# Four-layer attention and feed-forward kernel: the first feed-forward layer is computed in pieces inside the attention steps, through the two PSUM banks that the small products share

## The chip, the cores and the metric

The kernel runs on one core of a Trainium2 chip. The metric is the device time of one execution in microseconds (us). A core has a matrix engine (TensorE, PE in the profile, with its weight loads as PEld), VectorE (DVE), ScalarE (ACT), GpSimd (POOL) and SyncE (SP, which here issues all transfers). Each engine takes its own instructions strictly in order and waits on semaphores for the others. Matrix products land in PSUM, eight banks of 128 x 512 floats, and DVE or ACT take them out from there.

## The reference, cut to what matters

The input x has 4 batches of 512 tokens of 128 channels. Every layer adds an attention and then a feed-forward network to x, each on the layer norm of x:

```
x = x + attention0(norm(x))   # 16 heads of 8, keys: 154 of the context and 64 learned ones
x = x + ffn0(norm(x))
x = x + attention1(norm(x))   # keys and queries RMS-normalised, 154 keys
x = x + ffn1(norm(x))         # 4 experts of 512, gated
x = x + attention2(norm(x));  x = x + ffn2(norm(x))
x = x + attention3(norm(x));  x = x + ffn3(norm(x))

def ffn0(x):                  # per batch; m1, m2: outer products of 16 tokens' rows
    h = gelu(x @ (W1 + scale * m1(x)).T + b1)     # 128 -> 512
    return h @ (W2 + scale * m2(x)).T + b2        # 512 -> 128
```

The weights of ffn0 differ from batch to batch, because m1 and m2 are made of 16 token rows of the normalised x of that batch. What one batch does never depends on another batch.

## The kernel before

The work is a list of 32 items, layer by layer and batch by batch: four attention items A of layer 0, four of ffn0 (kind F0), four A of layer 1, four F1, four A of layer 2, four F2, A3, F3. In this text A0 to A3 are the attention items of layer 0, A4 to A7 those of layer 1, A8 to A11 those of layer 2, and F0_0 to F0_3 are the four batches of ffn0.

An item has slots (steps). An attention item has N = 28 slots in layer 0 and N = 20 in the layers 1 and 2, and four more in which its last products drain. In slot n `attention_step` has PE compute one block of transposed scores into bank 0 or 1 (L819), ACT takes its exp into a ring of eight (`exps`, L1534), and from slot 5 on PE runs, every fourth slot each, four products of the probabilities with the values into bank 6 (L830) and four for the denominators into bank 7 (L838). Scores of slot n wait for the exp of slot n-2, which read the same bank. At the end DVE takes a reciprocal and multiplies (`attention_end`), and the output product and its addition to x are the piece "finish", in slot 6 of the next item.

What else an item needs is done in pieces within the slots of the items ahead of it. `plan(i)` writes them down: `put(n, name, ...)` hangs a piece on slot n of item i, and every engine walks through the slots in order and, in a slot, first does the item's own step and then the slot's pieces in the order of the put calls. The pieces of this text: "ln" and "norm" (layer norm: statistics on DVE, the rest on POOL), "xt" (four PE transposes into bank 4, copied out by ACT, L698, L1445), "q", "q1" to "q4", "qsplit", "qlow" (query projection and its preparation; "q1" and "q3" on POOL, "q2" and "q4" on DVE), "kproj", "k1", "k2", "k3", "ksplit", "klow" (the same for the keys; "k2" on DVE, "k1", "k3", "klow" on POOL, "ksplit" on ACT), "kt" (transposes of the keys into the banks 4 and 5), "kb" (four ACT copies out of both banks, one per head of a group, L1426), "qxt" (four groups g of query transposes into bank 2 + g%2, each copied out by ACT, L720, L1473), "max" (32 score products m into bank 2 + m%2, each reduced by DVE, L736, L1118), "mt" (the transposed maxima), "v" (values, part 0 in bank 4 and part 1 in bank 5, masked out of PSUM by DVE). For each bank the builder keeps in `taken` which signal frees it. PE waits for that signal before the bank's next product, and all that stands behind it in PE's queue waits too.

```
            for h in range(HL):
                put(h, "kb", a1, h)
            for g in range(G):
                put(1 + g, "qxt", a1, g)
            for m in range(N_MAX):
                put(5 + m * (N - 4) // N_MAX, "max", a1, m)
```

An F0 item has 4 slots and 4 for the drain. "rows": SP copies the 16 rows of xn into `EV`/`OD` with four DMAs (`lora_dma`) and POOL spreads them (`lora_rows`). "late": PE makes m1 and m2 by two products into bank 5 (`lora`, L768), DVE adds each to the weights (L1192, L1194), ACT and DVE split the first into two parts of fp32r. Then `up` (three products per tile of 128 hidden channels, L874 to L876, into the banks 0 and 2), gelu on ACT (L1551), and `down` (16 products of 128 columns, L893, bank 6 or 7), which DVE adds to x (L1293). While the F0 items run, no attention item does: in their slots lie the preparation of A4 and A5 and all 32 "max" of A4.

Of the kernel before, what the change touches and what calls it, by code (L numbers as in the profile page):

```python
# [116 lines left out]

def plan(i):

# [9 lines left out]
    a = layer * B + b  # L129
    nxt = i + 1  # L130
    if i + 2 < len(ITEMS) and ITEMS[i + 2][0] == "A" and ITEMS[i + 2][2] == 0:
        put(0, "bv", ITEMS[i + 2][1])
    if i + 2 < len(ITEMS):
        for t in range(T):
            put(0 if kind in ("F0", "A3", "F3") else t, "ln", i + 2, t)
        put(0 if kind in ("F0", "A3", "F3") else 3, "norm", i + 2)
    if kind == "A":
        if is_attn(nxt):
            a1 = a + 1
            if b == 0:  # L140
                put(0, "kt", a1)
            for h in range(HL):
                put(h, "kb", a1, h)
            for g in range(G):
                put(1 + g, "qxt", a1, g)
            for m in range(N_MAX):
                put(5 + m * (N - 4) // N_MAX, "max", a1, m)
            put(6 + (N_MAX - MT_LAST) * (N - 4) // N_MAX, "mt", a1, 0)
            put(N + 1, "mt", a1, 1)
            put(N, "v", a1, 0)  # L150
            put(N + 1, "v", a1, 1)
        if is_attn(i + 2):
            put(N + 3, "kt", a + 2)
        if is_ffn(nxt):
            put(2, "xt", nxt)
            put(3, "after_xt", nxt)
            for n in range(3):
                put(5 + n, "late", nxt, n)
        if is_attn(i - 1):
            put(6, "finish", i - 1)  # L160
        if is_attn(i + 2):
            put(7, "xt", i + 2)
            put(9, "q", a + 2)
            for n, name in ((9, "q1"), (11, "q2"), (12, "q3"), (16, "q4"), (17, "qsplit"), (18, "qlow")):
                put(n, name, a + 2)
        if a + 2 < 12:
            put(10, "kproj", a + 2)
            for n, name in ((10, "k1"), (12, "k2"), (13, "k3"), (N - 2, "ksplit"), (N - 1, "klow")):
                put(n, name, a + 2)
        if i + 2 < len(ITEMS) and ITEMS[i + 2][0] == "F0":  # L170
            put(10, "rows", i + 2)
        if layer > 0:
            n_w = len(weight_chunks(layer))
            for c in range(b * n_w // B, (b + 1) * n_w // B):
                put(4 + 3 * (c - b * n_w // B), "w", layer, c)
    elif kind in ("F0", "F1", "F2"):
        short = kind == "F0"
        if is_attn(i - 1):
            put(2, "finish", i - 1)
# [22 lines left out]
        if is_attn(i + 2):  # L202
            a2 = ITEMS[i + 2][1] * B + ITEMS[i + 2][2]
            at = (3, 3, 3, 4, 4, 5, 6, 7) if short else (5, 6, 6, 7, 7, 8, 8, 9)
            for n, name in zip(at, ("xt", "q", "q1", "q2", "q3", "q4", "qsplit", "qlow")):
                put(n, name, i + 2 if name == "xt" else a2)
        if i + 2 < len(ITEMS) and ITEMS[i + 2][0] == "F0":
            put(N, "rows", i + 2)
# [1676 lines left out]
```

## Time and profile before

| | us |
|---|---|
| median of three runs (lowest, highest) | 1090.92 (1089.46, 1092.05) |
| the profiled execution, whole | 1092.3 |
| its span, first to last instruction | 1090.4 |
| PE busy in the span | 962.9 |
| DVE / ACT / POOL busy | 572.2 / 432.6 / 270.5 |
| first scores of A1 to first scores of A6 | 293.4 |

The profile is one execution seen instruction by instruction. A timeline row gives the start, the duration, the engine, the source line, what is written and read, how many instructions of one kind are merged, and, in brackets, how long the engine sat idle before and who released it. The duration of matrix products overlaps with that of the next ones, so what one costs is read from the distance of the starts. PEclk is the clock that TensorE was granted, 1.00 being 2.4 GHz; it has two levels, and a mean between 0.5 and 1.0 says what part of a stretch lay at the lower one, 1.2 GHz.

### The profile page before, as it was taken

What the parts mean: (1) busy time and instruction counts of PE and PEld (TensorE: products, weight loads), DVE (VectorE), ACT (ScalarE), POOL (GpSimd) and SP (SyncE); (2) the same over time, 40 slices, a digit from 0 to 9 for tenths busy, and PEclk for the clock granted to TensorE, in tenths of its full rate; (3) what the DMA queues carried; (4) which work ended last, traced back from release to release, by engine and by line L of the source; (5) the groups of instructions that cost most, each with busy time, mean ns of one, the idle gap of its engine ahead of it and who ended that gap; (6) DMA issues with size and microseconds to landing.
All of it is one profiled execution on the core that took longest, in us unless ns stands there. A gap on an engine that the chain in (4) does not pass through costs nothing. (4 is left out here: it accounts for less than half of the span.)

```text
span 1090.4 us, 15279 instructions
## 1 busy us (share of the span) xinstructions
PE 962.9 (88%) x5522; PEld 659.4 (60%) x5522; DVE 572.2 (52%) x1371; ACT 432.6 (40%) x777; POOL 270.5 (25%) x394
## 2 busy tenths in 40 slices
PE   2788989988689888899998889898899999999885
PEld 2544454335554443478887655444488888878783
DVE  3645555433355656455454636757453645444468
ACT  1355554442326554433333244654522423222340
POOL 7311212334425451311021023521200101010044
PEclk9989999787769999999999989989999999999997
DMA  5000000000010111000000020110000000000001
GB/s 142 4 2 13 1 15 2 13 8 10 1 63 8 33 33 32 1 22 1 1 1 1 1 73 21 39 40 15 19 1 1 1 1 1 1 1 1 1 1 39
DMA packets 27572, 18.09 MB, mean 17 GB/s; under 512 B 6221, under 2 KB 25770, under 8 KB 27370
## 3 DMA queue, kind: packets, MB, share of 16 engines
q1 hardware_dynamic: 27498, 17.12, 5.6%
q8 instruction: 45, 0.74, 0.3%
q14 instruction: 29, 0.24, 0.1%
HBM read 15.63 MB, written 1.05 MB: 15 GB/s over the span
## 5 line engine op out<-in xcount | busy, mean ns | idle before, releaser
L1118 DVE TENSOR_REDUCE mneg<-PS 128x2 f32<-128x308 f32 (+1 forms) x384 | 184.0, 517 | 161.6 <-PE PS L736 155.6
L1534 ACT ACTIVATE work<-PS 124x512 f32<-124x512 f32 (+1 forms) x272 | 160.4, 605 | 135.2 <-PE PS L819 134.4
L1266 DVE TENSOR_TENSOR work<-PS,work 128x512 f32<-128x512 f32 (+2 forms) x168 | 114.8, 685 | 175.5 <-PE PS L876 129.8
L1559 ACT ACTIVATE work<-PS 128x512 f32<-128x512 f32 (+2 forms) x168 | 100.1, 597 | 253.3 <-PE PS L876 240.9
L893 PEld LDWEIGHTS PS<-down_w,work 128*128 128x128 f32 (+2 forms) x1472 | 174.6, 193 | 6.2 <-DVE work L1266 1.3
L893 PE MATMUL PS<-down_w,work 128*128 128x128 f32 (+2 forms) x1472 | 174.8, 276 | 1.0 <-DVE work L1266 1.0
L874 PE MATMUL PS<-xh_sb,arena 128*128 128x512 f32 (+2 forms) x352 | 148.7, 422 | 10.4 <-DVE work L1266 9.6
L1629 POOL TENSOR_SCALAR rstd<-bn_mv 128x4 f32<-128x4 f32 x32 | 8.7, 271 | 537.7 <-DVE bn_mv L1038 537.6
L876 PE MATMUL PS<-xh_sb,arena 128*128 128x512 f32 (+2 forms) x352 | 141.7, 403 | 0.0
L875 PE MATMUL PS<-xl_sb,arena 128*128 128x512 f32 (+2 forms) x352 | 141.0, 400 | 0.0
L736 PE MATMUL PS<-kb_sb,qxt_sb 97*128 97x308 f32 x256 | 88.6, 394 | 19.6 <-DVE mneg L1118 14.9
L736 PEld LDWEIGHTS PS<-kb_sb,qxt_sb 97*128 97x128 f32 x256 | 47.1, 198 | 95.2 <-DVE mneg L1118 52.0
L874 PEld LDWEIGHTS PS<-xh_sb,arena 128*128 128x128 f32 (+2 forms) x352 | 65.6, 186 | 35.5 <-DVE work L1266 14.1
L830 PE MATMUL PS<-work,vb_sb 124*32 124x512 f32 (+1 forms) x544 | 76.7, 637 | 2.9 <-DVE work L1241 1.8
L819 PE MATMUL PS<-qxt_sb,kb_sb 101*124 101x512 f32 x160 | 72.4, 469 | 5.7 <-ACT work L1534 5.6
L876 PEld LDWEIGHTS PS<-xh_sb,arena 128*128 128x128 f32 (+2 forms) x352 | 65.5, 186 | 18.3
L838 PE MATMUL PS<-work,mv_sb 124*32 124x512 f32 (+1 forms) x544 | 74.6, 621 | 0.0
L875 PEld LDWEIGHTS PS<-xl_sb,arena 128*128 128x128 f32 (+2 forms) x352 | 65.9, 187 | 12.8
L1239 DVE RECIPROCAL work<-PS 128x512 f32<-128x512 f32 x12 | 40.3, 3357 | 41.0 <-PE PS L838 41.0
L1297 DVE SCALAR_TENSOR_TENSOR x_res<-PS,gates_sb,x_res 128x128 f32<-128x128 f32 x192 | 53.5, 339 | 5.9 <-PE PS L893 5.9
L736 PE MATMUL PS<-arena,qxt_sb 97*128 97x436 f32 x128 | 48.8, 423 | 7.2 <-DVE mneg L1118 6.1
L736 PEld LDWEIGHTS PS<-arena,qxt_sb 97*128 97x128 f32 x128 | 22.9, 189 | 51.1 <-DVE mneg L1118 33.7
(169 smaller groups left out, 1209.7 us busy)
## 6 DMA issues: line engine op xcount, KB each, us to landing
ctx_rep<-in_ctxT SPq DMA_DIRECT2D x12, 308.0 KB, 3.2
stage<-in_w SPq DMA_DIRECT2D x8, 256.0 KB, 3.6
stage<-in_wg SPq DMA_DIRECT2D x8, 176.0 KB, 2.4
stage<-in_wu SPq DMA_DIRECT2D x8, 176.0 KB, 2.9
x_res<-in_x SPq DMA_DIRECT2D x4, 256.0 KB, 4.0
down_w<-in_w SPq DMA_DIRECT2D x1, 1024.0 KB
down_w<-in_wd SPq DMA_DIRECT2D x8, 128.0 KB
out<-x_res SPq DMA_DIRECT2D x4, 256.0 KB, 2.3
```

The costliest lines, as they stand in the source:

```text
L736: pe.matmul(PS[:, bank, 0:w], QXT[0:KX_ROWS, a % 2, g, t * 128:(t + 1) * 128], KB(layer)[0:KX_ROWS, a % 2, g, f * w:(f + 1) * w], start=Tr ...
L819: pe.matmul(PS[0:rows, n % 2, :], KB(layer)[0:K_ALL, a % 2, g, c * rows:(c + 1) * rows], QXT[0:K_ALL, a % 2, g, :], start=True, stop=True) ...
L830: pe.matmul(PS[32 * g:32 * g + 32, 6, :], VB[0:rows, a % 2, c, g * 32:(g + 1) * 32], P[0:rows, (4 * c + g) % P_RING, :], start=(c == 0), s ...
L838: pe.matmul(PS[32 * g:32 * g + 32, 7, :], mask[0:rows, c, :], P[0:rows, (4 * c + g) % P_RING, :], start=(c == 0), stop=(c == chunks - 1)). ...
L874: pe.matmul(o, w[0], xH[:, i % 2, :], start=True, stop=False)
L875: pe.matmul(o, w[0], xL[:, i % 2, :], start=False, stop=False)
L876: pe.matmul(o, w[1], xH[:, i % 2, :], start=False, stop=True).then_inc(*sig["up"].mark((i, kt, m)))
L893: mm = pe.matmul(PS[:, bank, t * 128:(t + 1) * 128], HH[0:rows, bank - 6, j, t * 128:(t + 1) * 128], rhs, start=(j == 0), stop=(j == len(t ...
L1118: dve.tensor_reduce(mneg[:, a % 2, t, h0:h0 + 2], PS[:, mx_bank(i_main, m), 0:2 * (KT0 if layer == 0 else KC)].rearrange("p (h n) -> p h n ...
L1266: dve.tensor_tensor(HH[0:rows, e % 2, j, :], PS[0:rows, 2 * (n % 2) + 1, :], SS[0:rows, n % 2, :], ALU.mult).then_inc(*sig["h"].mark((i, n)))
L1534: act.activation(P[0:rows, n % P_RING, :], PS[0:rows, n % 2, :], ACT.Exp, scale=SCALE).then_inc(*sig["p"].mark((i, n)))
L1559: act.activation(SS[0:rows, n % 2, :], PS[0:rows, bank, :], ACT.Silu).then_inc(*sig["act"].mark((i, n)))
```

## The change

The F0 items vanish from the walk (`MAIN` is the list of items without them) and their work becomes pieces of attention slots. For the batch b: "ln" and "norm" in the slots 9 and 10, "rows" in 13, "xt" in 16, "late" in 20 of the item A(b+1); "up0" (one tile each, into bank 4 or 5) in its slots N and N+1, one later for b = 3; "down0" (one quarter each, into bank 5) in the slots 1 to 4 and "acc0" in slot 4 of A(b+2). The layer norm of A(4+b) follows in the slots 4 and 5 of A(b+2), its "xt" in 9, "q" and "q1" in 11, "q2", "q3" in 16, "q4" in 20. In the items A2 to A5 the key pieces "k2" and "k3" go from 12 and 13 to 15 and 16, "ksplit" and "klow" from N-2 and N-1 to N and N+1. A3 now prepares A4 as every attention item prepares the next.

In all attention items that are followed by another, of every layer, "kb" goes from the slots 0 to 3 to the slots 0, 0, 1, 1, and "qxt" from the slots 1 to 4 to 2, 3, 5, 6. "max" stays from slot 5 on.

Buffers are made apart so that both can run: hidden layer `HH0`, `LW` for m1's sum, `EO` and `EBD` for the rows; `W1E` moves within the arena; the two buffers of the layer norm are dealt by the new order (`ring`) rather than by the item number's parity. The loads of later weights are issued at other items, and DMA scratch is set to 1024.

```diff
+    if is_attn(nxt):
+        a1 = a + 1
+        if a in (0, 2 * B):
+            put(0, "kt", a1)
+        for h in range(HL):
+            put(h // 2, "kb", a1, h)
+        for g in range(G):
+            put((2, 3, 5, 6)[g], "qxt", a1, g)
+        first = 5
+        for m in range(N_MAX):
+            put(first + m * (N + 1 - first) // N_MAX, "max", a1, m)
...
+        put(N + 1, "mt", a1, 1)
+        put(N, "v", a1, 0)
+        put(N + 1, "v", a1, 1)
+    if is_attn(nxt2):
+        put(N + 3, "kt", a + 2)
...
+    if is_attn(after(i, -1)):
+        put(6, "finish", after(i, -1))
+    for b0 in range(B):
+
+        j = B + b0
+        for t in range(T):
+            put_later(b0 + 1, 9, "ln", j, t)
+        put_later(b0 + 1, 10, "norm", j)
+        put_later(b0 + 1, 13, "rows", j)
+        put_later(b0 + 1, 16, "xt", j)
+        put_later(b0 + 1, 17, "after_xt", j)
+        put_later(b0 + 1, 20, "late", j, 0)
+        for n in range(4):
+            put_later(b0 + 1, n_slots(item_of(b0 + 1)) + (b0 == 3) + n // 2, "up0", j, n)
+        for t in range(T):
+            put_later(b0 + 2, 1 + t, "down0", j, t)
+        put_later(b0 + 2, 4, "acc0", j)
+        n = B + b0
+        for t in range(T):
+            put_later(b0 + 2, 4, "ln", item_of(n), t)
+        put_later(b0 + 2, 5, "norm", item_of(n))
+        for x, name in ((9, "xt"), (11, "q"), (11, "q1"), (16, "q2"), (16, "q3"), (20, "q4"), (21, "qsplit"), (22, "qlow")):
+            put_later(b0 + 2, x, name, item_of(n) if name == "xt" else n)
...
+        put(10, "kproj", a + 2)
+        for n, name in ((10, "k1"), (15 if shared else 12, "k2"), (16 if shared else 13, "k3"), (N if shared else N - 2, "ksplit"), (N + 1 if shared else N - 1, "klow")):
+            put(n, name, a + 2)
...
+            def up0(i, n):
+
+                b, bank = ITEMS[i][2], 4 + n % 2
+                if n == 0:
+                    pe.wait_ge(*sig["xl"].at(i))
+                    pe.wait_ge(*sig["lora_l"].at(i))
+                pe.wait_ge(*taken[bank])
+                cols = slice(n * 128, (n + 1) * 128)
+                pe.matmul(PS[:, bank, :], W1E[:, b % 2, 0, cols], xH[:, i % 2, :], start=True, stop=False)
+                pe.matmul(PS[:, bank, :], W1E[:, b % 2, 0, cols], xL[:, i % 2, :], start=False, stop=False)
+                pe.matmul(PS[:, bank, :], W1E[:, b % 2, 1, cols], xH[:, i % 2, :], start=False, stop=True).then_inc(*sig["up"].mark((i, n, 0)))
+                taken[bank] = sig["h_gelu"].at((i, n))
+
+            def down0(i, t):
+
+                b = ITEMS[i][2]
+                if t == 0:
+                    pe.wait_ge(*sig["h_gelu"].at((i, 3)))
+                    pe.wait_ge(*sig["lora_w"].at((i, 1)))
+                    pe.wait_ge(*taken[5])
+                for j in range(4):
+                    mm = pe.matmul(PS[:, 5, t * 128:(t + 1) * 128], HH0[:, j, t * 128:(t + 1) * 128], W2E[:, b % 2, j * 128:(j + 1) * 128],
+                                   start=(j == 0), stop=(j == 3))
+                if t == T - 1:
+                    mm.then_inc(*sig["y"].mark((i, 0)))
+                    taken[5] = sig["resid"].at(i)
...
+            def accumulate0(i):
+
+                b = ITEMS[i][2]
+                dve.wait_ge(*sig["y"].at((i, 0)))
+                dve.wait_ge(*sig["bias_in_x"].at(i))
+                xb = x[:, b * T:(b + 1) * T, :]
+                dve.tensor_tensor(xb, PS[:, 5, :].rearrange("p (t n) -> p t n", t=T), xb, ALU.add).then_inc(*sig["resid"].mark(i))
...
+            def gelu(i, n):
+
+                act.wait_ge(*sig["up"].at((i, n, 0)))
+                if n == 0:
+                    act.wait_ge(*sig["w_ffn0_in"].at(0))
+                    if ITEMS[i][2] > 0:
+                        act.wait_ge(*sig["y"].at((i - 1, 0)))
+                act.activation(HH0[:, n, :], PS[:, 4 + n % 2, :], ACT.Gelu, bias=b1T[:, n:n + 1]).then_inc(*sig["h_gelu"].mark((i, n)))
```

## Rows read from the trace of the kernel before

**Rows 1.** The page: busy time of the matrix engine, its share and instructions.

```profile
PE 962.9 (88%) x5522; PEld 659.4 (60%) x5522; DVE 572.2 (52%) x1371; ACT 432.6 (40%) x777; POOL 270.5 (25%) x394
```

**Rows 2.** Windows: A1, A2, A3, F0 with A4's preparation, A4, A5.

```profile
core 0: us, PE busy (x) PEld busy (x) DVE busy (x) ACT busy (x) POOL busy (x), PEclk, DMA share, GB/s
...
102.58:148.93 46.35, 42.69 (x258) 21.32 (x256) 26.92 (x48) 23.61 (x43) 7.39 (x9) 0.96 0.03 8
148.93:192.18 43.25, 39.35 (x237) 18.77 (x236) 26.41 (x49) 22.19 (x40) 12.56 (x24) 1.00 0.03 7
192.18:228.70 36.52, 33.30 (x164) 10.74 (x160) 11.47 (x19) 17.54 (x33) 12.89 (x24) 0.81 0.03 10
228.70:322.73 94.03, 71.79 (x313) 51.17 (x309) 41.29 (x95) 27.45 (x43) 35.24 (x52) 0.74 0.03 7
322.73:359.68 36.95, 34.71 (x200) 19.01 (x200) 20.71 (x54) 20.25 (x37) 19.15 (x38) 0.91 0.14 50
359.68:395.95 36.27, 32.49 (x202) 16.89 (x200) 24.14 (x55) 20.14 (x37) 19.10 (x38) 1.00 0.08 25
```

**Rows 3.** Timeline of PE in the F0 stage: down, up, the two `lora` products.

```profile
244.54 3.73 PE L893 MATMUL PS<-down_w,work 128*128 128x128 f32 x32
248.03 0.48 PE L874 MATMUL PS<-xh_sb,arena 128*128 128x512 f32 x1
...
248.90 1.12 PE L768 MATMUL PS<-stage,qb_sb 4*128 4x512 f32 x2
251.25 1.12 PE L768 MATMUL PS<-stage,qb_sb 4*128 4x512 f32 x2 [1.24 <-DVE qa_sb L1192]
252.31 0.50 PE L874 MATMUL PS<-xh_sb,arena 128*128 128x512 f32 x1
```

**Rows 4.** Timeline of PE at the head of A5: slots 0, 5, 7.

```profile
359.68 0.71 PE L819 MATMUL PS<-qxt_sb,kb_sb 101*124 101x512 f32 x2
...
365.70 1.06 PE L830 MATMUL PS<-work,vb_sb 124*32 124x512 f32 x8
366.70 0.41 PE L736 MATMUL PS<-kb_sb,qxt_sb 97*128 97x308 f32 x1
...
369.44 0.48 PE L819 MATMUL PS<-qxt_sb,kb_sb 101*124 101x512 f32 x1
```

**Rows 5.** Timeline of PE: transposes, and the product that needs ACT's copy of them.

```profile
293.97 0.63 PE L698 MATMUL PS<-ident_sb,xn_sb 128*128 128x128 f32 x4 [0.24 <-DVE mneg L1118]
295.38 2.05 PE L708 MATMUL PS<-w_attn,xt_sb 128*128 128x128 f32 x8 [0.78 <-ACT xt_sb L1445]
```

**Rows 6.** Timeline of ACT at the head of A5.

```profile
360.69 0.77 ACT L1426 ACTIVATE kb_sb<-PS,maskk_sb 97x616 fp32r<-97x616 f32 x1
...
361.82 0.79 ACT L1426 ACTIVATE kb_sb<-PS,maskk_sb 97x616 fp32r<-97x616 f32 x1
```

**Rows 7.** Timeline of DVE: last seed of "q2" in A4; first "max" in A5.

```profile
343.23 0.19 DVE L428 TENSOR_SCALAR q_rr_sb<-q_ms_sb 128x64 int32<-128x64 int32 x1
...
367.15 0.48 DVE L1118 TENSOR_REDUCE mneg<-PS 128x2 f32<-128x308 f32 x1 [2.28 <-PE PS L736]
```

**Rows 8.** Timeline of POOL: `lora_rows` in F0; end of "k3" in A4; norm in A5.

```profile
256.09 1.03 POOL L1735 TENSOR_TENSOR stage<-qb_sb,eye_sb 4x512 f32<-4x512 f32 x1 [5.02 <-DMA qb_sb<-xn_sb]
...
353.73 0.20 POOL L1686 COPY kx_sb<-kbias 77x8 f32<-77x8 f32 x1
...
364.96 0.23 POOL L1629 TENSOR_SCALAR rstd<-bn_mv 128x4 f32<-128x4 f32 x1 [9.11 <-DVE bn_mv L1038]
...
367.51 1.04 POOL L1636 TENSOR_TENSOR xn_sb<-xn_sb,rstd 128x512 f32<-128x512 f32 x1
```

**Rows 9.** Timeline of ACT: the switch from exp to gelu.

```profile
228.98 1.28 ACT L1551 ACT_TABLE_LOAD   x1 [2.19 <-PE PS L838]
230.28 0.69 ACT L1551 ACTIVATE work<-PS,b1t 128x512 f32<-128x512 f32 x1
```

**Rows 10.** Timeline of PE at the head of A6, which starts at 395.95.

```profile
404.51 0.55 PE L736 MATMUL PS<-kb_sb,qxt_sb 97*128 97x308 f32 x2
```

More of the change, by code:

```diff
@@ L65, with after, norm_order, ring @@
 ITEMS = [(kind, n // 2, b) for n, kind in enumerate(KINDS) for b in range(B)]
+MAIN = [i for i, item in enumerate(ITEMS) if item[0] != "F0"]
+def after(i, n):
+    p = MAIN.index(i) + n
+    return MAIN[p] if 0 <= p < len(MAIN) else None
 def is_attn(i):
-    return 0 <= i < len(ITEMS) and ITEMS[i][0] == "A"
+    return i is not None and ITEMS[i][0] == "A"
 def is_ffn(i):
-    return 0 <= i < len(ITEMS) and ITEMS[i][0] != "A"
+    return i is not None and ITEMS[i][0] != "A"
+def norm_order():
+    shared = [j for b in range(B - 1) for j in (B + 1 + b, 2 * B + b)]
+    return list(range(B + 1)) + shared + list(range(3 * B - 1, len(ITEMS)))
+NORMS = norm_order()
+def ring(j):
+    return NORMS.index(j) % 2
+def ring_before(j):
+    n = NORMS.index(j)
+    return NORMS[n - 2] if n >= 2 else None
 def item_of(a):
@@ L128, in plan @@
     N = n_slots(i)
[L129 to L133, printed above, removed]
-        for t in range(T):
[L135 to L179, printed above, removed]
@@ L180, in plan @@
+    nxt, nxt2 = after(i, 1), after(i, 2)
+    if is_attn(nxt2) and ITEMS[nxt2][2] == 0:
+        put(0, "bv", ITEMS[nxt2][1])
+    if nxt2 is not None:
+        for t in range(T):
+            put(0 if kind in ("A3", "F3") else t, "ln", nxt2, t)
+        put(0 if kind in ("A3", "F3") else 3, "norm", nxt2)
+    if kind in ("F1", "F2"):
+        if is_attn(after(i, -1)):
+            put(2, "finish", after(i, -1))
         if is_attn(nxt):
@@ L201, in plan @@
             put(N + 4, "scores3", nxt)
[L202 to L208, printed above, removed]
+        if is_attn(nxt2):
+            a2 = ITEMS[nxt2][1] * B + ITEMS[nxt2][2]
+            for n, name in zip((5, 6, 6, 7, 7, 8, 8, 9), ("xt", "q", "q1", "q2", "q3", "q4", "qsplit", "qlow")):
+                put(n, name, nxt2 if name == "xt" else a2)
     elif kind == "A3":
@@ L590, in _ @@
                     load(WF3[:, 2 * D:2 * D + E3], A["wgate3"], "w_ffn3_in", 0)
-                if kind == "A" and b == 0 and layer > 0:
-                    sp.wait_ge(*sig["resid"].at(i - 1))
+                if i in (item_of(B + 2), item_of(2 * B)):
+                    sp.wait_ge(*sig["resid"].at(2 * B - 1 if layer == 1 else i - 1))
                     if layer == 1:
@@ L903, in ffn_step @@
                     up(i, n)
-                if n < 4 and carries_on(i - 1):
+                if n < 4 and after(i, -1) is not None and carries_on(after(i, -1)):
                     downs(i - 1, n + len(tiles))
@@ L1001, in _ @@
             maxima_transposed(None, 0, 1)
-            for i in range(len(ITEMS)):
+            for i in MAIN:
                 kind = ITEMS[i][0]
@@ L1252, in ffn_step @@
                 tiles = ffn_tiles(kind)
-                if n < len(tiles) and kind != "F0":
+                if n < len(tiles):
                     e, col, rows, slot = tiles[n]
@@ L1280, in accumulate @@
                 kind, layer, b = ITEMS[i]
-                bank = 6 + (b if kind == "F0" else e) % 2
+                bank = 6 + e % 2
                 dve.wait_ge(*sig["y"].at((i, e)))
@@ L1383, in _ @@
                     v_mask(0, 1)
-            for i in range(len(ITEMS)):
+            for i in MAIN:
                 kind = ITEMS[i][0]
@@ L1451, in x_high @@
                         act.wait_ge(*sig["y"].at((j - 2, ffn_tiles(ITEMS[j][0])[-1][0])))
-                    act.activation(xH[:, j % 2, :], xT[:, j % 2, :], ACT.Copy).then_inc(*sig["xh"].mark(j))
+                    act.activation(xH[:, j % 2, :], xT[:, ring(j), :], ACT.Copy).then_inc(*sig["xh"].mark(j))
             def q_split(a):
@@ L1604, in _ @@
             mt_out(None, 0, 1)
-            for i in range(len(ITEMS)):
+            for i in MAIN:
                 kind = ITEMS[i][0]
@@ L1610, in _ @@
                         exps(i, n)
-                    elif kind in ("F0", "F1", "F2") and n < n_slots(i):
+                    elif kind in ("F1", "F2") and n < n_slots(i):
                         ffn_step(i, n)
@@ L1802, in _ @@
             pool.tensor_tensor(gq[:, 0, :], gq[:, 0, :], gq[:, 1, :], ALU.mult).then_inc(*sig["gkq_ready"].mark(0))
-            for i in range(len(ITEMS)):
+            for i in MAIN:
                 total, pieces = all_slots(i)
```

235 lines of the change are left out of this document (134 added, 101 removed).

## The prediction

> **What bounds the kernel now.** I read the page first: PE is busy for 88% of the span and no other engine for more than 52% [rows 1], so PE's queue sets the pace, and what counts is what stands in it. The windows by stage show where it doesn't flow. A1 and A2 take 46.35 and 43.25 us, A4 and A5 about 36.5, with PE busy for about nine tenths and near the full clock. The stretch that holds the four F0 items and A4's preparation takes 94.03 us, PE busy for 71.79 of them at a mean clock of 0.74, and A3, which prepares no attention item, 36.52 us at 0.81 [rows 2]. That is the money in the change: from A1's first scores to A6's first scores pass 395.95 - 102.58 = 293.4 us [rows 2]. The timelines of PE, ACT, DVE and POOL at an item's head and in the F0 stage then give prices and who waits for whom. They also show that the head of every attention item is set by ACT: between the first scores of A5 and its first products with the values lie 6.02 us (359.68 to 365.70) [rows 4].
>
> **Removed and added, A1 to A6.** The new chain holds five attention items and no F0 item. A1 keeps 46.35. A2 gets a query projection, its transposes and one "kt" more. I take 1.9 of the 3.1 us by which A1 is longer, since part of these is A1's clock of 0.96: 45.1. A3 becomes like A2, with layer 1's narrower maxima (128 of 436 columns fewer at 2.4 GHz: 0.05 us, 32 times) and fewer value products: 42, between 36.5 (as now) and 45.1. A4 and A5 go by A5: 36.3 each [rows 2]. Sum 206.0.
>
> F0's products move into them. Per batch: one set of transposes 0.4 (their row lasts 0.63 [rows 5], and overlaps), two `lora` products at 1.06 (251.25 to 252.31), four up tiles at 0.8 (three products with the change of kind: 0.87, from 248.03 to 248.90), down 3.5 (244.54 to 248.03) [rows 3]. That is 0.4 + 2.1 + 3.2 + 3.5 = 9.2, four times: 36.8.
>
> Then the waits, which are new because PE can't pass them:
> - `lora`: both products use bank 5, and the second starts 2.35 us after the first (248.90 to 251.25), 1.3 more than its price [rows 3]. DVE in turn waits inside "late" for the second product and for ACT's copy, and meanwhile takes out no maxima. PE has two banks of them ahead and then stands for about 1.1. Together 2.4, four times: 9.6.
> - Tail: up tile 0 needs bank 4, which "v" has just filled and DVE must empty, and tile 3 bank 5 likewise. A DVE exit takes 0.45 from the product's start to its own (366.70 to 367.15) [rows 4, 7] and then its duration. The products of the drain hide part: 1.3, four times: 5.2. Behind it wait "kt" and the next head.
> - Head with down0: it stands in slot 1 and needs bank 5, free only when the fourth "kb" is out. ACT does an exp and a copy in about 1.15 (360.69 to 361.82) [rows 6]; two exps, four copies and the start make some 4 us, in which PE has nothing but two scores. Behind down0 stand all further scores. Waiting 4.4, then 5.1 of work (down 3.5, scores and two groups of "qxt" 1.6), and 1.8 because it starts at 1.2 GHz: 11.3, against 6.0 now and 3.5 of down. Makes 1.8, four times (A2 to A5): 7.2.
> - POOL: in A2, A3 and A4 the norm of F0's batch starts after slot 9. Its four SP transfers leave when xn is done (3.6 us from 364.96 to 367.51 + 1.04), and POOL waits in "rows" for them (5.02 in the row) before it makes the 2.3 us of rows [rows 8]. "q1" and the bias lie in the wait; "k1" stands behind. From slot 9: 1.6 of statistics (estimated, four small pairs) + 3.6 + 3.7 for four transfers + 2.3 + 0.6 = 11.8, DVE's statistics delayed by 0.6: 12.4. DVE comes to "k2" in slot 15 after about 9.9 and waits 2.5; its maxima stand behind it, and PE after its two banks: 2.0, three times: 6.0. The transfers' place in SP's queue is free: what stands behind (the maxima's rows, the next context) is due ten slots later.
> - K in A5: from the seed of "q2" to the end of "k3" POOL needs 10.5 us (343.23 to 353.73 + 0.20) [rows 7, 8]. The seeds come five slots later than now, about 7, and A5's "kt" had about 3.5 to spare: 3.5, once.
>
> **The moved head pieces** act in ten items: A0 to A6 and A8 to A10. Group 2 of "qxt" now stands in slot 5 ahead of the first "max", and both use bank 2; group 3 stands in slot 6 behind the second "max", and both use bank 3. Counted from the start of the value products, A5 reaches slot 7's scores after 3.74 (365.70 to 369.44) [rows 4]. New: 1.0 values; then transposes, ACT's copy and the max that needs the bank, 1.4 as from transposes to their reader [rows 5]; max 0 starts at 2.4, max 1 and the scores follow. Group 3 waits for DVE's two reductions, 0.45 + 2 x 0.48 + 0.05 = 1.45 [rows 4, 7]: 3.85. Max 2 at 4.2, max 3 in bank 3 waits for the copy, another 1.4: 5.25; "finish" 0.8; slot 7's scores at 6.25. So 2.5 in the layers 1 and 2 (A4, A5, A6, A8 to A10). In layer 0 max 3 lies in slot 7: 2.1 (A0 to A3). ACT's copies out of the head don't shorten it: the value products wait for the fourth exp, ahead of which stood three "kb" and two "qxt" and now stand four and one. Bounds: nothing, if the waits fell on others, and 2.8, two full chains of rows 5. Inside A1 to A6 that is 3 x 2.1 + 2 x 2.5 = 11.3, outside 2.1 + 4 x 2.5 = 12.1.
>
> **Clock.** A6's head, like A5's but with a stretch at 1.2 GHz, reaches its first maximum after 8.56 (395.95 to 404.51) against 7.02 (359.68 to 366.70) [rows 2, 4, 10]: 1.5 per stretch. The new heads, `lora` and "k2" leave PE idle for 1 to 4 us. I take six stretches more than now: 9, of which 6 inside; bounds 0 and 17 stretches, 25. By the Trainium skill ("TensorE: Matmul & The Clock Gate", Part 1) the throttled clock is the default state and only activity releases it; the trace agrees, with 0.74 in the F0 stage and 1.00 in A2 and A5 [rows 2].
>
> **Tables.** Gelu among exps makes 8 table loads instead of 2. The load takes 1.28, and the gelu starts 1.30 after it [rows 9]. Before gelu, ACT has no exp left and PE is at "v": hidden. Before exp it overlaps "kt", 0.3 shows, in the tail above; uncovered it would be 6 x 1.3 = 8. The Trainium skill ("ScalarE: Activation LUTs", What ACT_TABLE_LOAD costs) adds a drain and gives 2.66 us per switch; by that, six more would cost 16 us of ACT, and the row here shows half of it.
>
> Costed at nothing: buffers, `ring`, weight loads (each due items later), DMA scratch.
>
> **Sum.** Inside: 206.0 + 36.8 + 9.6 + 5.2 + 7.2 + 6.0 + 3.5 + 11.3 + 6 = 291.6 against 293.4: -1.8. Outside: 12.1 + 3 = 15.1. Together +13.3: span 1103.7. The profiled execution took 1092.3, 1.4 over the median of 1090.92, so the median becomes 1104.
>
> **Rivals.**
> - *The heads are free* (the other side). If the waits of "qxt" for banks 2 and 3 cost nothing, because they take slack that PE would lose anyway to ACT and DVE, 23.4 go: 1081, faster. It decides as soon as the ten items lose less than 1.0 us each. For it: PE already waits in heads. Against: these waits come after the value products, where PE gets through to slot 7 in 3.74 us now [rows 4]. 0.20.
> - *The lower clock spreads*: every head, `lora` and "k2" has its stretch, 17 instead of 6: 1104 + 16.5 = 1121. For it: 0.74 and 0.81 in the stages with waits; against: A5 rides over its 6.02 us head at 1.00 [rows 2]. 0.12.
> - *It cancels*: the queue waits (k2, K in A5, `lora`'s second half: 6 + 3.5 + 4.4 = 13.9) don't arise, since DVE and POOL are idle half the time: 1090. For it: POOL's busy share; against: it is order, not load, that holds them. 0.08.
> - The forecast: 0.60, with its own range of 1093 to 1115.
>
> Range: 1081 to 1121, from the first rival to the second, which leaves out about their outer halves. A difference of 0.2% is what a measurement of this kernel can tell from none. Faster 0.20, same 0.08, slower 0.72.
>
> **What would show it.** First scores of A1 to those of A6 near 292; the items A8 to A10 2.5 longer each, with PE's idle time before "max" put down to the copy of "qxt" and before "qxt" to the maxima; 8 table loads; about 4 us of idle PE before each down0; DVE idle before the key's mean square for POOL. If A8 to A10 keep their length, the first rival holds. If a single stage grows by over 10 us for a wait that is not named here, the sum is wrong.

## The result, and the profile after

The changed kernel takes 1130.67 us (median of four runs, 1128.18 to 1136.37) against 1090.86 of the kernel before in runs on the same chip: ratio 1.0373, 95% interval 1.0332 to 1.0414. It is slower, as forecast, but by 39.8 us instead of 13, and the time lies outside the range given (1081 to 1121). The profiled execution took 1136.4, with a span of 1134.6 against 1090.4: 44.2 more. It is the slowest of the four, so the lengths read from its trace hold some 4 us more than the medians do.

The page of the changed kernel, where the last line is the granted clock in 40 slices of the span:

```profile
span 1134.6 us, 15284 instructions
...
PE 989.3 (87%) x5522; PEld 670.5 (59%) x5522; DVE 573.5 (51%) x1371; ACT 445.1 (39%) x783; POOL 272.3 (24%) x394
...
PEclk9969788688878988989999988788899999999997
```

PE has the same 5522 instructions as in [rows 1] and is busy 26.4 us longer with them. The same instructions take longer, so the clock is the first suspect. ACT has six instructions more, the table loads.

Windows of the changed kernel from first scores to first scores: A0 to A6 one by one. Then from first exp to first exp, A9 alone, A0 to A6 together, and A8 to A10 together:

```profile
core 0: us, PE busy (x) PEld busy (x) DVE busy (x) ACT busy (x) POOL busy (x), PEclk, DMA share, GB/s
57.64:109.67 52.03, 48.05 (x252) 24.08 (x251) 21.67 (x42) 24.41 (x44) 7.38 (x9) 0.82 0.01 2
109.67:172.84 63.17, 56.30 (x283) 27.83 (x282) 31.42 (x61) 29.96 (x52) 14.73 (x16) 0.84 0.04 11
172.84:243.14 70.30, 59.98 (x310) 31.61 (x308) 35.44 (x68) 31.58 (x53) 23.56 (x43) 0.83 0.02 6
243.14:308.95 65.81, 56.83 (x293) 30.37 (x292) 30.57 (x68) 31.61 (x53) 24.14 (x43) 0.82 0.02 4
308.95:369.00 60.05, 49.70 (x254) 28.54 (x252) 29.95 (x68) 27.88 (x47) 26.72 (x45) 0.83 0.09 24
369.00:417.31 48.31, 36.95 (x234) 21.70 (x232) 28.69 (x58) 21.75 (x38) 17.88 (x37) 0.96 0.05 14
417.31:459.00 41.69, 37.57 (x181) 18.19 (x179) 17.28 (x44) 18.92 (x34) 10.82 (x14) 0.80 0.13 47
...
711.56:754.15 42.59, 37.64 (x199) 19.35 (x198) 24.09 (x51) 21.20 (x40) 15.72 (x19) 0.84 0.11 30
58.52:459.60 401.08, 345.19 (x1785) 182.34 (x1785) 194.53 (x399) 185.62 (x318) 125.24 (x207) 0.84 0.05 14
668.77:796.07 127.30, 110.98 (x562) 55.04 (x562) 63.17 (x137) 60.81 (x114) 37.60 (x45) 0.83 0.13 37
```

And three of these windows of the kernel before, again A9, A0 to A6, and A8 to A10:

```profile
680.50:716.37 35.87, 32.55 (x199) 16.89 (x198) 24.12 (x51) 20.88 (x41) 15.77 (x19) 1.00 0.13 36
57.68:432.66 374.98, 329.96 (x1785) 175.98 (x1785) 193.43 (x400) 173.50 (x312) 123.27 (x207) 0.89 0.05 15
642.03:753.22 111.19, 101.21 (x558) 50.38 (x558) 62.93 (x137) 60.09 (x113) 37.72 (x45) 0.92 0.15 42
```

A9 is the cleanest place to look. Nothing of the feed-forward layer is in it, and PE does the same 199 instructions, but it takes 42.59 us instead of 35.87, and the clock fell from 1.00 to 0.84. A length times twice what its PEclk lacks to 1.00 is the time at 1.2 GHz: 13.6 us in A9 after, none before. By the same product A0 to A6 went from 82 to 128 us at that level and A8 to A10 from 18 to 43. From the first scores of A1 to those of A6 pass 307.6 us, against 293.4 in [rows 2].

Timeline of PE in the changed kernel (L930 scores, L941 values, L800 "qxt", L816 "max"): first, from A2 and the end of A5, the places of the other terms; then, from 717.53 on, the moved head pieces in A9:

```profile
177.58 2.05 PE L905 MATMUL PS<-down_w,hidden 128*128 128x128 f32 x8 [4.02 <-ACT arena L1537]
...
208.18 0.47 PE L816 MATMUL PS<-arena,qxt_sb 97*128 97x436 f32 x1 [0.96 <-DVE mneg L1221]
...
209.75 0.73 PE L816 MATMUL PS<-arena,qxt_sb 97*128 97x436 f32 x1 [0.86 <-DVE mneg L1221]
...
217.71 2.07 PE L848 MATMUL PS<-lora_diag,lora_rows 4*128 4x512 f32 x2 [0.84 <-DVE lora_tmp L1295]
...
235.41 0.47 PE L892 MATMUL PS<-xh_sb,arena 128*128 128x512 f32 x1 [0.88 <-DVE vb_sb L1173]
...
416.60 0.91 PE L733 MATMUL PS<-ident_sb,kx_sb 77*97 77x77 f32 x8 [3.71 <-POOL kx_sb L1805]
...
717.53 1.94 PE L941 MATMUL PS<-work,vb_sb 124*32 124x512 f32 x8
719.40 1.17 PE L800 MATMUL PS<-ident_sb,qx_sb 128*97 128x128 f32 x4
721.35 0.85 PE L816 MATMUL PS<-kb_sb,qxt_sb 97*128 97x308 f32 x2 [0.78 <-ACT qxt_sb L1585]
722.00 0.63 PE L930 MATMUL PS<-qxt_sb,kb_sb 101*124 101x512 f32 x1
722.99 1.14 PE L800 MATMUL PS<-ident_sb,qx_sb 128*97 128x128 f32 x4 [0.37 <-DVE mneg L1221]
724.82 0.62 PE L816 MATMUL PS<-kb_sb,qxt_sb 97*128 97x308 f32 x1 [0.43 <-ACT qxt_sb L1585]
```

The three waits of the moved pieces are there and in the forecast order: a maximum waits for ACT's copy of group 2 (0.78 us idle), group 3 for DVE's maxima (0.37), a maximum for the copy of group 3 (0.43). But the eight value products take 1.94 us where those of [rows 4] take 1.06: this work, which no wait interrupts, runs at 1.2 GHz. Before down0 PE stands 4.02 us (forecast 4.4), the second `lora` product waits, and A6's "kt" waits 3.71 for POOL's keys (forecast 3.5).

The heads aren't the only places with the lower clock. Windows of the changed kernel: A1 at `lora`; A2 in its head, in what follows, and at "k2" with `lora`; A3 at "k2" with `lora`; A4 at `lora`:

```profile
148.00:155.50 7.50, 6.89 (x19) 2.30 (x23) 3.13 (x5) 2.16 (x4) 0.00 (x0) 0.54 0.00 0
172.84:183.00 10.16, 6.14 (x31) 5.51 (x30) 3.56 (x2) 6.00 (x10) 0.00 (x0) 0.66 0.01 2
183.00:209.00 26.00, 22.70 (x143) 12.33 (x141) 17.41 (x42) 11.88 (x22) 13.09 (x14) 1.00 0.00 1
209.00:227.00 18.00, 16.41 (x42) 5.40 (x42) 8.28 (x15) 5.17 (x9) 9.75 (x28) 0.53 0.00 0
281.00:295.50 14.50, 13.66 (x40) 4.40 (x32) 5.92 (x11) 4.33 (x8) 9.14 (x26) 0.53 0.00 1
355.50:364.00 8.50, 7.51 (x24) 2.98 (x22) 3.39 (x6) 3.31 (x7) 5.50 (x14) 0.60 0.00 0
```

In A2 the head holds 6.9 us at 1.2 GHz, and the stretch that starts in the waits behind "k2" and goes on through `lora` holds 16.9. Such stretches of A1 to A4 make 44 of the 92 us at the lower level in A1 to A5.

### The profile page after: what moved, and what is told of

Its sections match the earlier page's. It is cut to its first block and busy times, and to the rows that moved or that the text cites. A ratio compares the mean times of both kernels' runs of the same rounds, so it can differ in the third digit from the quotient of the medians.

```text
span 1134.6 us, 15284 instructions
## 1 busy us (share of the span) xinstructions
PE 989.3 (87%) x5522; PEld 670.5 (59%) x5522; DVE 573.5 (51%) x1371; ACT 445.1 (39%) x783; POOL 272.3 (24%) x394
## 5 line engine op out<-in xcount | busy, mean ns | idle before, releaser
L996 PEld LDWEIGHTS PS<-down_w,work 128*128 128x128 f32 (+2 forms) x1344 | 157.9, 191 | 5.7 <-DVE work L1380 1.3
L996 PE MATMUL PS<-down_w,work 128*128 128x128 f32 (+2 forms) x1344 | 158.3, 275 | 1.0 <-DVE work L1380 1.0
L980 PE MATMUL PS<-xh_sb,arena 128*128 128x512 f32 (+2 forms) x336 | 138.8, 413 | 9.9 <-DVE work L1380 9.9
L982 PE MATMUL PS<-xh_sb,arena 128*128 128x512 f32 (+2 forms) x336 | 133.5, 397 | 0.0
L981 PE MATMUL PS<-xl_sb,arena 128*128 128x512 f32 (+2 forms) x336 | 132.9, 396 | 0.0
L816 PE MATMUL PS<-kb_sb,qxt_sb 97*128 97x308 f32 x256 | 89.6, 395 | 24.5 <-DVE mneg L1221 12.6
L816 PEld LDWEIGHTS PS<-kb_sb,qxt_sb 97*128 97x128 f32 x256 | 47.6, 202 | 103.6 <-DVE mneg L1221 48.5
L930 PE MATMUL PS<-qxt_sb,kb_sb 101*124 101x512 f32 x160 | 75.2, 488 | 11.1 <-ACT work L1658 10.9
L941 PE MATMUL PS<-work,vb_sb 124*32 124x512 f32 (+1 forms) x544 | 82.0, 678 | 1.8 <-DVE work L1355 1.2
L949 PE MATMUL PS<-work,mv_sb 124*32 124x512 f32 (+1 forms) x544 | 81.5, 675 | 0.0
L980 PEld LDWEIGHTS PS<-xh_sb,arena 128*128 128x128 f32 (+2 forms) x336 | 61.5, 183 | 28.8 <-DVE work L1380 14.2
L982 PEld LDWEIGHTS PS<-xh_sb,arena 128*128 128x128 f32 (+2 forms) x336 | 61.5, 183 | 17.2
L981 PEld LDWEIGHTS PS<-xl_sb,arena 128*128 128x128 f32 (+2 forms) x336 | 61.7, 184 | 12.7
L816 PE MATMUL PS<-arena,qxt_sb 97*128 97x436 f32 x128 | 53.4, 458 | 9.5 <-DVE mneg L1221 6.4
L816 PEld LDWEIGHTS PS<-arena,qxt_sb 97*128 97x128 f32 x128 | 25.1, 207 | 55.4 <-DVE mneg L1221 30.8
L930 PE MATMUL PS<-qxt_sb,arena 101*125 101x512 f32 x112 | 54.9, 496 | 3.0 <-ACT work L1658 2.9
```

What stands on the lines that cost most here:

```text
L816: pe.matmul(PS[:, bank, 0:w], QXT[0:KX_ROWS, a % 2, g, t * 128:(t + 1) * 128], KB(layer)[0:KX_ROWS, a % 2, g, f * w:(f + 1) * w], start=Tr ...
L930: pe.matmul(PS[0:rows, n % 2, :], KB(layer)[0:K_ALL, a % 2, g, c * rows:(c + 1) * rows], QXT[0:K_ALL, a % 2, g, :], start=True, stop=True) ...
L941: pe.matmul(PS[32 * g:32 * g + 32, 6, :], VB[0:rows, a % 2, c, g * 32:(g + 1) * 32], P[0:rows, (4 * c + g) % P_RING, :], start=(c == 0), s ...
L949: pe.matmul(PS[32 * g:32 * g + 32, 7, :], mask[0:rows, c, :], P[0:rows, (4 * c + g) % P_RING, :], start=(c == 0), stop=(c == chunks - 1)). ...
L980: pe.matmul(o, w[0], xH[:, i % 2, :], start=True, stop=False)
L981: pe.matmul(o, w[0], xL[:, i % 2, :], start=False, stop=False)
```

## The experiments

The labels [E1] to [E12] are used below. "After" is the changed kernel; each ratio is against the kernel before, run in the same job.

**[E1] The new head order alone, in the kernel before.**

```diff
             for h in range(HL):
-                put(h, "kb", a1, h)
+                put(h // 2, "kb", a1, h)
             for g in range(G):
-                put(1 + g, "qxt", a1, g)
+                put((2, 3, 5, 6)[g], "qxt", a1, g)
```

> The kernel before with only the new order of the head pieces (kb in slots 0,0,1,1, qxt in 2,3,5,6), F0 stage untouched; nine items have it. Theory (the bank waits ahead of the maxima, and the lower clock that they bring): the lengths of A8 to A10 as in the changed kernel, 4 to 7 us more per item, so 1125 to 1140. Waits without a clock effect: 3 x 2.1 + 6 x 2.5 = 21 more, 1112. Rival (the heads are free, the loss is the F0 pieces'): 1091.

Measured: 1147.03 us against 1091.52, ratio 1.0529 (1.0473 to 1.0586), above the 1125 to 1140 that I expected. Nine heads have the new order here, and it alone costs 55.5 us. The whole change, with ten such heads, costs less, so what it does with the F0 items gives some 16 us back. A9 has the length that it has after:

```profile
722.59:765.00 42.41, 37.78 (x199) 19.65 (x198) 24.10 (x51) 21.18 (x40) 15.71 (x19) 0.84 0.11 30
...
728.56 1.94 PE L830 MATMUL PS<-work,vb_sb 124*32 124x512 f32 x8
```

**[E2] After, with all four "qxt" ahead of the maxima** (each `qxt` line in A0 to A6, A8 to A10).

```diff
-            put((2, 3, 5, 6)[g], "qxt", a1, g)
+            put((2, 3, 4, 4)[g], "qxt", a1, g)
```

> The changed kernel with qxt groups 2 and 3 both in slot 4, ahead of the first maximum, kb as changed. Theory (the waits of groups 2 and 3 around the first maxima cost 2.1 to 2.5 us per item in ten items, and more through the clock): 1095 to 1107. Rival (the lower clock comes from the idle time before the value products, which stays): at most 12 us less, 1118 or more. Rival (heads free): 1130.

Measured: 1097.9, ratio 1.006 (1.0034 to 1.0086). Moving group 2 by one slot and group 3 by two takes back 32.8 of the 39.8 us.

**[E3] After, with the old head where no down0 stands** (A0, A1, A6, A8 to A10).

```diff
+        down = 2 <= a <= B + 1
         for h in range(HL):
-            put(h // 2, "kb", a1, h)
+            put(h // 2 if down else h, "kb", a1, h)
         for g in range(G):
-            put((2, 3, 5, 6)[g], "qxt", a1, g)
+            put((2, 3, 5, 6)[g] if down else 1 + g, "qxt", a1, g)
```

> The changed kernel with the old head order in A0, A1, A6, A8, A9, A10 (the items without a down0), the new one only in A2 to A5. Theory: these six items return to their old lengths, 5 to 6 us each, 1095 to 1102; A8 to A10 as in the kernel before to 1 us. Rival (heads free): 1130.

Measured: 1094.33, ratio 1.0038 (1.0013 to 1.0062). Six heads give 36.3 us, 6.1 each, against 2.1 to 2.5 that I had priced for a head's waits. A9 is as it was in the kernel before: 35.86 us at 1.00.

**[E4] After, with the idle time of the heads filled.** The kernel also computes products of 128 x 512 that nobody reads: 14 behind slot 1's scores in A2 to A5, and in the other heads 4 behind slot 2 and 3 behind slot 3. No real wait is removed.

```diff
+            def fill(i, n):
+                a = ITEMS[i][1] * B + ITEMS[i][2]
+                w = KB(ITEMS[i][1])[0:K_ALL, a % 2, 0, 0:128]
...
+                for _ in range(count):
+                    pe.matmul(PS[:, bank, :], w, QXT[0:K_ALL, a % 2, 0, :], start=True, stop=True)
```

> The changed kernel with products whose result nobody reads in the head's idle time: fourteen behind slot 1 where a down0 waits, four behind slot 2 and three behind slot 3 elsewhere, each into a bank that is free there. They shorten no wait. Theory (a large part of the loss is the lower clock after idle heads): time at the lower clock in the attention items of layers 0 to 2 falls by half, 1105 to 1120. Rival (the waits alone cost, the clock little): 1130 or more, since 100 products are added.

Measured: 1107.61, ratio 1.0178 (1.0118 to 1.0238). More work, and 23.1 us less than after. In the windows A0 to A6 and A8 to A10 the time at 1.2 GHz falls from 172 to 77 us. Windows of A0 to A6 and of A9:

```profile
57.65:434.38 376.73, 334.59 (x1862) 181.31 (x1862) 194.74 (x402) 185.12 (x318) 124.99 (x207) 0.93 0.05 15
...
685.25:726.33 41.08, 37.04 (x206) 19.60 (x205) 24.13 (x51) 21.18 (x40) 15.73 (x19) 0.92 0.11 31
```

Two fillings don't keep the clock up everywhere, so this is only a lower bound of what the clock costs.

**[E12] The head order alone as in [E1], each head filled with 16 unread products** (four behind slot 2, three behind slot 3, two behind slot 4, four between the third group and the first maximum, three behind slot 6's scores).

```diff
+                        if n == 6:
+                            fill(i, 4, 3)
...
+                        if kind == "A" and n == 5 and p[0] == "qxt":
+                            fill(i, 4, 4)
+                    if kind == "A" and n in (2, 3, 4):
+                        fill(i, {2: 3, 3: 6, 4: 4}[n], {2: 4, 3: 3, 4: 2}[n])
```

> The kernel before with the new head order (1147) and 16 products that nobody reads in each of the nine heads: 4 behind slot 2, 3 behind 3, 2 behind 4, 4 between the third group of qxt and max 0, 3 behind the scores of slot 6, while PE would wait. No wait is shorter. Theory (21 of the 56 us are the waits, the rest is the lower clock after them): the time at the lower clock in A0 to A10 falls from 204 us to the 108 of the kernel before or less, and the time to 1108 to 1120. Rival (the waits are longer than worked out, and the clock costs little): 1140 or more.

Measured: 1112.70 against 1090.07, ratio 1.0206 (1.0179 to 1.0233). A9, the window and the head:

```profile
697.28:735.84 38.56, 36.30 (x215) 19.34 (x214) 24.09 (x51) 21.19 (x40) 15.74 (x19) 1.00 0.12 33
...
702.95 1.06 PE L841 MATMUL PS<-work,vb_sb 124*32 124x512 f32 x8
```

This is the cleanest split. At 1.00 the new order costs A9 38.56 - 35.87 = 2.7 us, which is the waits (2.5 forecast). A2 and A5, at 1.00 in both kernels too, grow by 2.6 (45.88 against 43.27) and 2.75 (39.02 against 36.27). The same order unfilled costs another 42.41 - 38.56 = 3.9, which is the clock. Over nine heads: 22.6 us of waits (the forecast's prices give 3 x 2.1 + 6 x 2.5 = 21.3), and 55.5 - 22.6 = 32.9 of clock, 3.7 per head. The totals are less clean than the item. The fillers may lengthen a head a little themselves; then the waits are smaller and the clock's part larger. Against that, [E12] has only 79 us at 1.2 GHz in A0 to A6 and A8 to A10 (from the clock of these two windows, as above), the kernel before 100 and [E1] 192. So part of the 32.9 repays a lower clock that the kernel before had as well, and the 22.6 hide some 6 us of waits (21 us at 0.28, the price worked out below).

**[E11] Only "kb" moved, in the kernel before** (the first line of [E1]'s edit).

> The kernel before with only kb moved to the slots 0,0,1,1, qxt left in 1 to 4. Theory (the 56 us of the head order come from qxt around the maxima, with the clock): within 9 of the kernel before, 1091 to 1100. Rival (kb ahead of the exps delays the value products and brings the lower clock by itself): more than half of the 56, 1119 or more.

Measured: 1101.99, ratio 1.0102 (1.0075 to 1.0129), just above the 1091 to 1100 expected. So of the 55.5 us some 12 come from two copies per slot, which lie ahead of the exps on ACT, and some 44 from "qxt"; that edit moves all four groups, but [E2] gets 32.8 us back from the groups 2 and 3 alone. I had priced the copies at nothing. In A9 of this run the value products start 6.85 us behind the first scores (682.44), against 6.02 in the kernel before, and then run at 1.2 GHz:

```profile
687.33 0.65 PE L720 MATMUL PS<-ident_sb,qx_sb 128*97 128x128 f32 x4 [1.36 <-ACT qxt_sb L1473]
...
689.29 1.94 PE L830 MATMUL PS<-work,vb_sb 124*32 124x512 f32 x8
```

**[E5] The best heads**: [E3] with the order of [E2] in A2 to A5.

```diff
-            put((2, 3, 5, 6)[g] if down else 1 + g, "qxt", a1, g)
+            put((2, 3, 4, 4)[g] if down else 1 + g, "qxt", a1, g)
```

> The two gains put together: old head order in the items without down0, and in A2 to A5 kb in slots 0,0,1,1 and qxt in 2,3,4,4, ahead of the first maximum. Theory: the run with the old heads (1094) less what A2 to A5 gained by qxt ahead of the maxima (3.3 + 3.7 + 3.9 + 0.2): 1083, below the kernel before. Rival (the F0 pieces as such cost as much as the stage did): 1090 or more.

Measured: 1088.88, ratio 0.9981 (0.9956 to 1.0006). That is 5.5 us below [E3] instead of 11, between what I expected and the rival; down0 still leaves PE idle in slot 1 (4.03 us in A2).

**[E6] The same, the second `lora` product in bank 4.**

```diff
...
-                    pe.wait_ge(*taken[5])
-                    pe.matmul(PS[:, 5, :], OD[:, n, :], EBD[:, n, :], start=True, stop=True).then_inc(*sig["lora_psum"].mark((j, n)))
-                    taken[5] = sig["lora_w"].at((j, n))
+                    pe.wait_ge(*taken[5 - n])
+                    pe.matmul(PS[:, 5 - n, :], OD[:, n, :], EBD[:, n, :], start=True, stop=True).then_inc(*sig["lora_psum"].mark((j, n)))
+                    taken[5 - n] = sig["lora_w"].at((j, n))
...
-                dve.scalar_tensor_tensor(W2E[:, b % 2, :], PS[:, 5, :], scale0[:, :], W2T, ALU.mult, ALU.add).then_inc(*sig["lora_w"].mark((j, 1)))
+                dve.scalar_tensor_tensor(W2E[:, b % 2, :], PS[:, 4, :], scale0[:, :], W2T, ALU.mult, ALU.add).then_inc(*sig["lora_w"].mark((j, 1)))
```

> As the run with the best heads, and the second lora product goes to bank 4, so that it doesn't wait for DVE. Theory (that wait costs 1.3 us of PE and a part of DVE's time, four times): 5 less than the run with the best heads, 1078. Rival (DVE sets the end of late anyway, PE waits for maxima instead): no change, 1083.

Measured: 1078.28, ratio 0.990 (0.9874 to 0.9925); 10.6 less than [E5]. That the expected 1078 came out is luck, since it stood for 5 us below an expected 1083. Both products (two instructions each) now stand in one row with no wait between them, and A0 to A6 take 358.80 us:

```profile
196.02 2.21 PE L849 MATMUL PS<-lora_diag,lora_rows 4*128 4x512 f32 x4
...
57.59:416.39 358.80, 314.17 (x1785) 171.30 (x1785) 193.50 (x402) 183.17 (x317) 125.74 (x207) 0.93 0.05 15
```

The whole `lora` term of the prediction was 9.6, and only its second half goes here.

**[E7] [E5] with A5's keys early**: there "k2", "k3", "ksplit", "klow" in their old slots.

```diff
+        late = shared and a != B + 1
-        for n, name in ((10, "k1"), (15 if shared else 12, "k2"), (16 if shared else 13, "k3"), (N if shared else N - 2, "ksplit"), (N + 1 if shared else N - 1, "klow")):
+        for n, name in ((10, "k1"), (15 if late else 12, "k2"), (16 if late else 13, "k3"), (N if late else N - 2, "ksplit"), (N + 1 if late else N - 1, "klow")):
```

> As the run with the best heads, and in A5, where no F0 batch is prepared, k2, k3, ksplit and klow stand in their old slots 12, 13, N-2, N-1. Theory (kt waits for POOL's late key chain): A5 3.5 us shorter, 1079.5. Rival (kt then waits for something else): A5's length unchanged.

Measured: 1082.98, ratio 0.9939 (0.9914 to 0.9963). A5 falls from 47.78 us in [E5] to 42.74; its term was 3.5.

**[E8] After, with down0 out of the head and the old heads everywhere**: down0 in the slots 4 to 7, "acc0" and "ln" in 7, "finish" and "norm" in 8, "xt" in 12, "q" and "q1" in 13.

```diff
...
-            put_later(b0 + 2, 1 + t, "down0", j, t)
-        put_later(b0 + 2, 4, "acc0", j)
+            put_later(b0 + 2, 4 + t, "down0", j, t)
+        put_later(b0 + 2, 7, "acc0", j)
...
```

> The changed kernel with down0 in slots 4 to 7 and acc0 in 7, finish in 8, the next norm, xt and q one to three slots later, so that all items keep the old head order. Theory (PE's 4 us of waiting for bank 5 ahead of each down0, and the lower clock that follows, are the largest loss left in A2 to A5): 6 to 7 us less for each of these four than with the old heads elsewhere, 1066 to 1072. Rival (down0 among the maxima displaces as much as the wait cost): 1083 or more.

Measured: 1081.69, ratio 0.9925 (0.9901 to 0.9949). The wait is gone, the clock is not: in A2 down0 finds its bank after 0.50 us, but its eight products still take 2.05 us, as with the 4.02 us wait.

```profile
166.92 2.05 PE L905 MATMUL PS<-down_w,hidden 128*128 128x128 f32 x8 [0.50 <-ACT arena L1537]
```

It gains 12.6 us over [E3], not the 22 to 28 that I expected, and part of that is the head order, which goes back in A2 to A5 too. Against [E5], where "qxt" stands ahead of the maxima, it gains 7.2. What holds the clock down in these heads although down0 no longer waits was not isolated.

**[E10] and [E9]: everything together.** [E10] is [E5] with the edits of [E6] and [E7]; [E9] is [E8] with both.

> The best heads (down0 in slots 1 to 4) with both other corrections, second lora product in bank 4 and A5's keys early. Theory: 1088.9 - 10.6 - 5.9 = 1072; A2 to A4 still 4 us idle before down0.

> down0 in slots 4 to 7 with the old heads, and besides the second lora product in bank 4 and A5's keys early. Theory (the three losses are separate): 1081.7 - 10.6 - 5.9 = 1065. If they overlap, down to 1075.

Measured: [E10] 1075.76, ratio 0.987 (0.9844 to 0.9895). [E9] 1068.46, ratio 0.9798 (0.9768 to 0.9828), 2.0% faster than the kernel before and the fastest of all. Both lie 3 to 4 us above the sums of the single gains. Windows of [E9]: A5, A0 to A6, A8 to A10.

```profile
336.88:376.41 39.53, 35.26 (x229) 20.00 (x227) 24.50 (x56) 20.14 (x37) 18.40 (x38) 1.00 0.04 16
57.59:411.37 353.78, 319.77 (x1785) 169.85 (x1785) 194.82 (x402) 181.62 (x317) 124.83 (x207) 0.92 0.05 16
619.10:729.80 110.70, 101.38 (x558) 49.88 (x558) 62.89 (x137) 60.13 (x113) 37.69 (x45) 0.92 0.15 42
```

A0 to A6 take 21.2 us less than before with the same products on PE, and A8 to A10 have their old length. So computing F0 within the attention items pays: with the old heads outside A2 to A5 the kernel is within 0.4% of the one before ([E3], [E5]), each of the three waits eased by itself puts it 0.6 to 1.0% below ([E6], [E7], [E8]), and all of them 2.0%.

One warning on single items: A9 has the same head and the same products in the kernel before, [E3], [E5], [E6] and [E8], at 1.00 and 35.9 us, and in [E7] and [E9], at 0.91 and 38.2 us. What decides this was not isolated. A difference of 2 us in one item of one trace proves nothing; the medians and several items together do.

## Why the forecast had the sign and missed the size

**The step that failed is "Clock".** I took six further stretches at 1.2 GHz, at 1.5 us each: 9. In its place the profiled execution shows some 38. What the five items inside and the five outside show over the forecast's other terms:

| | forecast without clock | after | difference |
|---|---|---|---|
| A1: 46.35 + 0.4 + 2.1 + 3.2 + 2.4 + 1.3 + 2.1 | 57.9 | 63.17 | 5.3 |
| A2: 45.1 + 9.2 + 2.4 + 1.3 + 1.8 + 2.0 + 2.1 | 63.9 | 70.30 | 6.4 |
| A3: 42 + the same | 60.8 | 65.81 | 5.0 |
| A4: 36.3 + the same, head 2.5 | 55.5 | 60.05 | 4.6 |
| A5: 36.3 + 3.5 + 1.8 + 3.5 + 2.5 | 47.6 | 48.31 | 0.7 |
| A0, A6, A8 to A10, growth | 12.1 | 28.3 | 16.2 |

Together 38.2 instead of 9. The last row's 28.3 is 6.6 (A0), 5.6 (A6) and 16.1 (A8 to A10). The largest differences stand where the clock is 0.80 to 0.84; in A5, at 0.96, it is 0.7. The time at the lower level, priced by [E12], gives about the same size in its own way. A9 loses 3.9 us for 13.6 at 1.2 GHz, 0.28 per us, and the whole of [E1] against [E12] 32.9 for 112, 0.29. A1 to A5 have 88 us more at that level than the rows from which I took their lengths, the items outside 51 more than in the kernel before: at 0.28 that is 25 and 14, together 39 (an estimate). So most of the table's differences is the clock's; errors of the other terms, which go both ways, are in it too.

The number was wrong in both factors. Not six stretches came but one in all ten heads (A5's only 3.4 us long; A0, A6, A8 and A10 had a shorter one before) and another in each of A1 to A4, where `lora` and "k2" stand; by time these four are nearly half of what A1 to A5 have. And a stretch doesn't end with the head. I had read A6's from its start to the first maximum, 1.5 us longer than A5's [rows 4, 10]; it was 3.4 us long in all, as this window of the kernel before shows (A6 is at 1.00 ahead of it and behind it):

```profile
400.50:405.00 4.50, 3.85 (x16) 1.72 (x16) 0.60 (x5) 4.12 (x9) 3.54 (x5) 0.62 0.00 0
```

In A9 after, 13.6 us of 42.59 lie at 1.2 GHz, and the head is 6.5. The products behind it go on slowly. That a us at the lower level costs less than half a us I put down to work that waits for other engines anyway; no run tests this. The rival "the lower clock spreads" had the right mechanism, and nearly the count, but the same 1.5, and so its 1121 fell short too. By the Trainium skill ("TensorE: Matmul & The Clock Gate", Part 1) the throttled clock is the default and activity releases it; [E4] and [E12] agree, where unread products bring A9 from 0.84 to 0.92 and 1.00.

**The moved head pieces: right.** Forecast 2.5 for A9 and A5, measured 2.7 and 2.75; forecast 2.1 for A2, measured 2.6. The rival "the heads are free" is refuted by this. That 22.6 for nine heads comes so near the 21.3 of the forecast is partly luck, as said at [E12]. One cause inside it was missed: "kb" alone, costed at nothing, is worth 12 us [E11], waits and clock together.

**down0 in the head: right**, 4.02 us of wait for 4.4. In A2 the values start 12.5 us behind the first scores (172.84 to 185.36) for 11.3. Moving it behind the first maxima gives 7.2 us ([E5] to [E8]) and 7.3 ([E10] to [E9]), and the term was 7.2. The order of "kb" and "qxt" in A2 to A5 goes back in the same step, so the two aren't fully apart. My expectation for [E8] had counted much more.

**`lora`: the right place, too small.** Idle 0.84 before the second product. Its second half alone gives 10.6 us, about 5 of it by my price. Between [E5] and [E6] the clock of A0 to A6 rises from 0.91 to 0.93, 16 us less at 1.2 GHz, which at 0.28 is the other 5 (an estimate; no filled run separates the two).

**Tail: right.** 0.88 before an up tile for "v" being taken out; 1.3 priced, two tiles together. In A4 it is 1.48, and for a gelu.

**POOL's queue and "k2": wrong.** I had "k1" behind "rows". It stands in slot 10, behind the norm and ahead of "rows", so DVE waits for nothing at "k2". POOL and DVE in A2 of the changed kernel:

```profile
203.03 0.61 POOL L1765 TENSOR_TENSOR ka_sb<-k_sb 77x256 f32<-77x256 f32 x1
...
205.28 1.03 POOL L1845 TENSOR_TENSOR lora_diag<-lora_rows,eye_sb 4x512 f32<-4x512 f32 x1 [0.64 <-DMA lora_rows<-xn_sb]
```

```profile
205.28 0.41 DVE L1155 TENSOR_REDUCE k_ms_sb<-ka_sb 77x32 f32<-77x256 f32 x1
...
206.38 1.22 DVE L507 TENSOR_SCALAR k_rr_sb<-k_ms_sb 77x32 int32<-77x32 int32 x1
207.52 0.60 DVE L1221 TENSOR_REDUCE mneg<-PS 128x2 f32<-128x436 f32 x1
...
209.09 1.12 DVE L1221 TENSOR_REDUCE mneg<-PS 128x2 f32<-128x436 f32 x2
```

POOL waits 0.64 us for the transfers instead of 5.02 [rows 8]. What PE does lose there are the rows at 208.18 and 209.75 above, 0.96 and 0.86: one reduction stands behind 2.2 us of DVE's own key work (205.28 to 207.52), the next behind 1.1 of its query work. These 1.8 us are near the 2.0 of the term by luck; the longest such wait in A3 and A4 is 0.8. What was left over of the 6.0 hid part of the clock's error.

**K in A5: right.** 3.71 idle for 3.5; moving it gives 5.0 in A5, whose clock rises from 0.93 to 0.96, and 5.9 in the total [E7].

**Tables: right.** Six more loads, and the exp behind one starts 0.3 us later after the first scores than before. ACT in the changed kernel:

```profile
172.39 1.28 ACT L1658 ACT_TABLE_LOAD   x1 [0.46 <-PE PS L949]
173.69 0.60 ACT L1658 ACTIVATE work<-PS 125x512 f32<-125x512 f32 x1
```

The first scores of A2 start at 172.84, so the exp comes 0.85 behind them. The Trainium skill ("ScalarE: Activation LUTs", What ACT_TABLE_LOAD costs) gives 2.66 us per switch with a drain; here the activation starts 1.30 us after the start of its load, and no drain shows.
